# Another split of the C products between VectorE and GpSimd, stage by stage, in a Mamba, expert and recurrence block

## The reference

```python
def step(h, t):
    u_t, d_t, B_t, C_t = t
    dA = jnp.exp(d_t[:, :, None] * A)
    h = dA * h + (d_t * u_t)[:, :, None] * B_t[:, None, :]
    y_t = jnp.einsum('bdn,bn->bd', h, C_t)
    return (h, y_t)
```

## Time and profile before

| | |
|---|---|
| median of 3 runs | 1953.68 us (1950.45 to 1956.26) |
| profiled execution, its time | 1957.38 us |
| profiled execution, its span | 1955.6 us |
| VectorE busy | 1661.3 us (85% of the span) |
| TensorE busy | 1608.4 us (82%) |
| ScalarE busy | 1537.7 us (79%) |
| GpSimd busy | 1358.5 us (69%) |
| granted TensorE clock, mean | 0.938 of full |

### The profile page before, as it was taken

One profiled execution on the slowest core, in us unless ns is written; L12 is line 12 of the kernel. 1 busy time (PEld: TensorE's weight loads), 2 busy tenths in 40 slices (PEclk: granted clock), 3 DMA queues, 4 the chain that ended last, 5 costly groups with the idle time before them and its releaser, 6 DMA issues. The chain is left out here.

```text
span 1955.6 us, 24773 instructions
## 1 busy us (share of the span) xinstructions
PE 1608.4 (82%) x6097; PEld 887.0 (45%) x6186; DVE 1661.3 (85%) x4204; ACT 1537.7 (79%) x3276; POOL 1358.5 (69%) x1209
## 2 busy tenths in 40 slices
PE   5788788879898988898898989898989986766653
PEld 2333344445454545454454545454545443444332
DVE  3889989899998999999999999999999998844431
ACT  5666778789897979898898989898998975465543
POOL 0234647488877787787778788777778777776665
PEclk8899899999999999999999999999999997997776
DMA  2000212023323223232323232322323232233232
GB/s 60 11 11 27 71 29 70 27 79 86 88 83 93 81 79 96 76 98 81 93 84 90 84 99 79 92 87 67 103 81 95 83 85 83 76 102 98 87 95 83
DMA packets 79901, 151.06 MB, mean 77 GB/s; under 512 B 20584, under 2 KB 46592, under 8 KB 79680
## 3 DMA queue, kind: packets, MB, share of 16 engines
q0 software_dynamic: 49152, 134.28, 24.0%
q1 hardware_dynamic: 29344, 14.65, 2.7%
q10 hardware_dynamic: 1248, 0.34, 0.1%
HBM read 145.01 MB, written 4.19 MB: 76 GB/s over the span
## 5 line engine op out<-in xcount | busy, mean ns | idle before, releaser
L1468 POOL DMA_INDIRECT rows<-in_experts,index x1024 | 981.9, 959 | 357.2 <-issue 288.8
L1354 DVE TENSOR_TENSOR_SCAN hp<-dA,fed_ps 128x1024 f32<-128x1024 f32 x256 | 583.7, 2280 | 7.7 <-issue 2.9
L784 PE MATMUL ysum<-hp,ident 128*128 128x512 f32 x1024 | 487.6, 621 | 4.0 <-DVE hp L1364 3.4
L1483 POOL TENSOR_TENSOR hp<-hp,c_row 128x1024 f32<-128x1024 f32 x112 | 264.8, 2364 | 219.7 <-ACT c_row L1044 178.0
L1027 ACT ACTIVATE dA<-delta,decay 128x511 f32<-128x511 f32 x512 | 334.7, 711 | 17.2 <-issue 15.4
L1338 DVE TENSOR_TENSOR fed_ps<-du,b_ps 128x1024 f32<-128x1024 f32 x256 | 313.7, 1225 | 39.2 <-PE b_ps L759 23.5
L1006 ACT ACTIVATE rows<-rows,coef 128x128 f32<-128x128 f32 x1024 | 311.1, 390 | 13.1 <-DVE coef L1274 13.1
L784 PEld LDWEIGHTS ysum<-hp,ident 128*128 128x128 f32 x1024 | 206.7, 202 | 219.4 <-issue 201.7
L934 ACT ACT_TABLE_LOAD x218 | 279.7, 1283 | 8.8 <-PEq L544 5.0
L717 PE MATMUL bank<-rows,ident 128*128 128x256 f32 x1024 | 251.2, 402 | 32.5 <-ACT rows L1006 32.5
L1267 DVE CUSTOM_DVE_ANT_0 rows<-rows,xn 128x128 f32<-128x128 f32 x1024 | 240.9, 298 | 39.5 <-DMA rows<-in_experts,index 39.1
(11 more groups left out here) (182 smaller groups left out, 2195.4 us busy)
## 6 DMA issues: line engine op xcount, KB each, us to landing
rows<-in_experts,index POOLq DMA_INDIRECT x1024, 2.7
x_in<-in_x SPq DMA_DIRECT2D x16, 256.0 KB, 4.1
x_res<-in_x SPq DMA_DIRECT2D x16, 256.0 KB, 4.7
y<-x SPq DMA_DIRECT2D x16, 256.0 KB, 2.7
rows<-in_taps SPq DMA_DIRECT2D x1, 512.0 KB
rows<-in_wq_t SPq DMA_DIRECT2D x1, 512.0 KB, 5.2
rows<-in_in_proj_t ACTq DMA_DIRECT2D x1, 256.0 KB
rows<-in_key_t SPq DMA_DIRECT2D x1, 128.0 KB, 5.2
```

The costliest lines, as they stand in the source:

```text
L784: mm = nc.tensor.matmul(ysum[:, j, :], ident[:], hp[:, BUFFER[k], j, :], start=(k == SUM_ORDER[0]), stop=(k == SUM_ORDER[-1]))
L1354: nc.vector.tensor_tensor_scan(flat, dA[:, n % NDA, :, :].rearrange("p a b -> p (a b)"), fed_ps[:].rearrange("p a b -> p (a b)"), 0.0, ALU ...
L1468: pool.indirect_dma_start(e.rows[:, t, h, :], None, A["experts"], bass.IndirectOffsetOnAxis(ap=e.index[:, t, h:h + 1], axis=0)).then_inc(e ...
L1483: pool.tensor_tensor(state, state, c_row[:, k % NCR, :].unsqueeze(1).to_broadcast([P, NH, T]), ALU.mult).then_inc(pool_read, 1)
```

## The change

The set of states whose product GpSimd forms becomes a function of the stage, on_pool(c). In stage 0 it holds 1 to 14; in stage 1 it is 3, 4, 5, 7, 8, 9, 11; in stage 2 it is 1, 3, 5, 7, 8, 9, 11; in stage 3 it is 1, 3, 5, 6, 7, 8, 9, 11, 13; in stage 15 it is 1, 3, 5, 7, 9; in stages 4 to 14 it stays as it was. The order of the y sums follows the set of the stage, and the counts on which engines wait are added up over the stages. Slots, buffers and all other steps stay.

```diff
 POOL_STATES = (1, 3, 5, 7, 9, 11, 13)
-DVE_STATES = tuple(n for n in range(NS) if n not in POOL_STATES)
-
-SUM_AT = [min(n + 1 + (n in POOL_STATES), NS - 1) for n in range(NS)]
-SUM_ORDER = sorted(range(NS), key=lambda n: (SUM_AT[n], n))
...
+POOL_AT = {0: (1, 2, 3, 4, 5, 6, 7, 8, 9, 10, 11, 12, 13, 14), 1: (3, 4, 5, 7, 8, 9, 11), 2: (1, 3, 5, 7, 8, 9, 11), 3: (1, 3, 5, 6, 7, 8, 9, 11, 13), 15: (1, 3, 5, 7, 9)}
+
+def on_pool(c):
+
+    return POOL_AT.get(c, POOL_STATES) if isinstance(c, int) else POOL_STATES
+
+def pool_count(c, n):
+
+    if isinstance(c, int):
+        earlier = sum(len(on_pool(k)) for k in range(c))
+    else:
+        earlier = c * len(POOL_STATES) + sum(len(on_pool(k)) - len(POOL_STATES) for k in range(LOOP_FROM))
+    return earlier + sum(k <= n for k in on_pool(c))
...
+def sum_at(c, n):
+
+    return min(n + 1 + (n in on_pool(c)), NS - 1)
+
+def sum_order(c):
+
+    return sorted(range(NS), key=lambda n: (sum_at(c, n), n))
...
         def multiplied(c, n):
 
-            if n in POOL_STATES:
-                return pool_read, at(c, len(POOL_STATES), POOL_STATES.index(n))
-            return read_out, at(c, len(DVE_STATES), DVE_STATES.index(n))
+            if n in on_pool(c):
+                return pool_read, pool_count(c, n)
+            return read_out, dve_count(c, n)
...
-                        for k in [x for x in SUM_ORDER if SUM_AT[x] == n]:
+                        order = sum_order(c)
+                        for k in [x for x in order if sum_at(c, x) == n]:
                             pe.wait_ge(*multiplied(c, k))
...
-                        if n in POOL_STATES:
-                            c, k = b[CORE], POOL_STATES.index(n)
+                        if n in on_pool(b[CORE]):
+                            c = b[CORE]
                             act.wait_ge(c_spread, at(c, NS, n))
 
-                            if k >= NCR:
-                                act.wait_ge(pool_read, at(c, len(POOL_STATES), k - NCR))
-                            elif later(c):
-                                act.wait_ge(pool_read, at(c - 1, len(POOL_STATES), len(POOL_STATES) + k - NCR))
-                            nc.scalar.activation(c_row[:, k % NCR, :], c_ps[:, 0, :],
+                            if later(c) or n > on_pool(c)[0]:
+                                act.wait_ge(pool_read, pool_count(c, n) - NCR)
+                            nc.scalar.activation(c_row[:, 0, :], c_ps[:, 0, :],
                                                  ACT.Copy).then_inc(c_kept, 1)
...
-                    if CORE in has and part == 2 and n in DVE_STATES:
+                    if CORE in has and part == 2 and n not in on_pool(b[CORE]):
...
-                    if CORE in has and part == 0 and n in POOL_STATES:
-                        c, k = b[CORE], POOL_STATES.index(n)
+                    if CORE in has and part == 0 and n in on_pool(b[CORE]):
+                        c = b[CORE]
                         pool.wait_ge(scanned, at(c, NS, n))
-                        pool.wait_ge(c_kept, at(c, len(POOL_STATES), k))
+                        pool.wait_ge(c_kept, pool_count(c, n))
```

More of the change, by code:

```diff
@@ L223, with dve_count, summed @@
 POOL_STATES = (1, 3, 5, 7, 9, 11, 13)
-DVE_STATES = tuple(n for n in range(NS) if n not in POOL_STATES)
-SUM_AT = [min(n + 1 + (n in POOL_STATES), NS - 1) for n in range(NS)]
-SUM_ORDER = sorted(range(NS), key=lambda n: (SUM_AT[n], n))
-def summed(n):
-    return SUM_ORDER.index(n)
+POOL_AT = {0: (1, 2, 3, 4, 5, 6, 7, 8, 9, 10, 11, 12, 13, 14), 1: (3, 4, 5, 7, 8, 9, 11), 2: (1, 3, 5, 7, 8, 9, 11), 3: (1, 3, 5, 6, 7, 8, 9, 11, 13), 15: (1, 3, 5, 7, 9)}
[7 more added lines that the diff above has]
+    return earlier + sum(k <= n for k in on_pool(c))
+def dve_count(c, n):
+    if isinstance(c, int):
+        earlier = sum(NS - len(on_pool(k)) for k in range(c))
+    else:
+        earlier = c * (NS - len(POOL_STATES)) + sum(len(POOL_STATES) - len(on_pool(k)) for k in range(LOOP_FROM))
+    return earlier + sum(k not in on_pool(c) for k in range(n + 1))
+def sum_at(c, n):
+    return min(n + 1 + (n in on_pool(c)), NS - 1)
+def sum_order(c):
+    return sorted(range(NS), key=lambda n: (sum_at(c, n), n))
+def summed(c, n):
+    return sum_order(c).index(n)
 def offset(phase, slot):
@@ L604, in multiplied @@
         def multiplied(c, n):
-            if n in POOL_STATES:
-                return pool_read, at(c, len(POOL_STATES), POOL_STATES.index(n))
-            return read_out, at(c, len(DVE_STATES), DVE_STATES.index(n))
+            if n in on_pool(c):
+                return pool_read, pool_count(c, n)
+            return read_out, dve_count(c, n)
         def c_used(c, n):
-            if n in POOL_STATES:
-                return c_kept, at(c, len(POOL_STATES), POOL_STATES.index(n))
+            if n in on_pool(c):
+                return c_kept, pool_count(c, n)
             return multiplied(c, n)
@@ L784, in iteration @@
                                 mm = nc.tensor.matmul(ysum[:, j, :], ident[:], hp[:, BUFFER[k], j, :],
-                                                      start=(k == SUM_ORDER[0]), stop=(k == SUM_ORDER[-1]))
+                                                      start=(k == order[0]), stop=(k == order[-1]))
                             mm.then_inc(y_sum, 1)
@@ L1350, in iteration @@
                         if before:
-                            dve.wait_ge(y_sum, at(c, NS, summed(before[-1])))
+                            dve.wait_ge(y_sum, at(c, NS, summed(c, before[-1])))
                         elif later(c):
-                            dve.wait_ge(y_sum, at(c - 1, NS, summed(max(k for k in range(NS) if BUFFER[k] == BUFFER[n]))))
+                            last = max(k for k in range(NS) if BUFFER[k] == BUFFER[n])
+                            dve.wait_ge(y_sum, at(c - 1, NS, summed(c - 1, last)))
                         nc.vector.tensor_tensor_scan(flat, dA[:, n % NDA, :, :].rearrange("p a b -> p (a b)"),
@@ L1477, in iteration @@
                     n, part = divmod(slot, TURN // NS)
-                    if CORE in has and part == 0 and n in POOL_STATES:
-                        c, k = b[CORE], POOL_STATES.index(n)
+                    if CORE in has and part == 0 and n in on_pool(b[CORE]):
+                        c = b[CORE]
                         pool.wait_ge(scanned, at(c, NS, n))
-                        pool.wait_ge(c_kept, at(c, len(POOL_STATES), k))
+                        pool.wait_ge(c_kept, pool_count(c, n))
                         state = hp[:, BUFFER[n], :, :]
                         pool.tensor_tensor(state, state,
-                                           c_row[:, k % NCR, :].unsqueeze(1).to_broadcast([P, NH, T]),
+                                           c_row[:, 0, :].unsqueeze(1).to_broadcast([P, NH, T]),
                                            ALU.mult).then_inc(pool_read, 1)
```

## The result

The changed kernel takes 1991.75 us in the median of 6 runs (1986.43 to 1997.19); the kernel before beside it takes 1956.6 (6 runs, 1950.45 to 1963.17). The ratio is 1.0154, 95% interval 1.0114 to 1.0193: 1.5% slower, against a forecast of 1940 us.

The account below looks back on a forecast made before the run. VectorE was taken to bound stages 0 to 3, while GpSimd can hold up work in stage 15. Stage terms -4.7 - 5.0 - 1.7 + 0 - 2.4 sum to -13.8 us, giving 1940 us; range 1930 to 1952.

Parts of the forecast that it names:

- Stages 4 to 14: Stages whose product set is unedited: assumed to keep their time, so no term in the sum.
- Stage 0, -4.7: Stage 0: seven products move to GpSimd; five count at 0.95 us each, -4.7 us; bounds 0 and -8.5.
- the 6.6 of all seven products: Stage 0: saving if all seven moved products kept their 0.95 us each; the forecast said not all stays.
- not 5: Stage 0, sign of a right forecast: the scan of state 15 comes some 5 us earlier.
- the early wait for b_ps: Stage 0: the feed's 3.73 us wait for TensorE's b_ps would lengthen by what products 2 and 4 save.
- Stages 1 and 2, -5.0 and -1.7: Moving product 13 to VectorE ends GpSimd collisions; stage 1 also shortens its tail: -5.0 us, and -1.7 in stage 2.
- Stage 3, 0: Products 6 and 8 to GpSimd: saving swallowed by a later b_ps wait, 0 us; bounds -1.9 and +1.2.
- Stage 15, -2.4: Products 11 and 13 to VectorE: +1.1, collision gone -2.7, shorter y-sum wait -0.8, so -2.4 us; GpSimd's lead becomes idle.
- rival (a): GpSimd's stage 15 lead carries through the drain: -9.5 instead of -2.4, -20.9 in all, 1932.8 us; chance 0.18.
- -13.8: Sum over stages 0, 1, 2, 3 and 15: -4.7 - 5.0 - 1.7 + 0 - 2.4 us.
- Rival (b): TensorE and ScalarE swallow VectorE's savings; only three collisions go: -4.9 us, 1948.8 us; chance 0.20.
- Rival (c): Slower: ScalarE's copies wait on the one C row in stages 0 and 3: +10.2 us, 1964; chance 0.09.

Follow-up runs that it names:

- e5: Changed kernel plus four tiny ScalarE copies at the start, its loop at place 813 instead of 808: 1953.5 us, ratio 0.9925 to the kernel before.
- e7: Kernel before plus seventeen tiny ScalarE copies at the start, its loop at 808 instead of 790, no product moved: 1995.7 us, ratio 1.0196.
- e1: Changed kernel with the second expert layer's first weigh one slot earlier in stages up to 14: 1962.4 us, ratio 0.999 to the kernel before.
- e9: Kernel before (old sets) with the weigh one slot earlier and twenty-two ScalarE copies, loop at 813: 1956.3 us.
- e12: Changed kernel (all new sets) with the weigh one slot earlier and four ScalarE copies, loop at 813: 1940.3 us.
- e11: Changed kernel with stage 3's old set, the weigh one slot earlier and eight ScalarE copies, loop at 813: 1994.4 us.
- e3: Kernel before with only stage 15's new set: 1968.1 us, ratio 0.9996 to the kernel before.
- e10: Kernel before with stage 15's new set alone, the weigh one slot earlier and twenty-two ScalarE copies, loop at 813: 1958.0 us.
- e6: Changed kernel with four ScalarE copies at the start and the weigh one slot earlier: 1938.4 us, ratio 0.9878 to the kernel before.
- e13: e11 with four tiny VectorE memsets at the start, VectorE's loop at 1090 instead of 1086: 1940.8 us, ratio 0.9864 to the kernel before.
- e14: e12 with four tiny VectorE memsets at the start, VectorE's loop at 1086 instead of 1082: 1997.5 us, ratio 1.0149 to the kernel before.

## Why the prediction was wrong

**Stages 4 to 14.** The failed step is the sentence that they keep their set "and, I take it, their time". It was never worked out; no rival had it. They lost 59 us in all: 63.8 in stages 6 to 13, with 4.7 gained in the others. Two things did it, neither of them a wait on the change's data. Nine more c_row copies in stages 0 and 3 made ScalarE's code 18 instructions longer ahead of the loop, which put the place of a second fetch on the first dA behind each jump (e5, e7). And the weigh met GpSimd's product (e1), by what trigger stays open. The prediction counted the copies' 0.58 us and not their code.

**Stage 0, -4.7.** From first scan to first scan 78.2 became 71.3, -6.9 (-6.1 between e9 and e12): about the 6.6 of all seven products. Two lines of DVE of after carry it:

```profile
107.53 2.29 DVE L1384 TENSOR_TENSOR_SCAN hp<-dA,fed_ps 128x1024 f32<-128x1024 f32 x1
...
114.48 1.23 DVE L1367 TENSOR_TENSOR fed_ps<-du,b_ps 128x1024 f32<-128x1024 f32 x1 [3.34 <-POOL du L1534]
```

The scan of state 15 begins 7.7 us earlier than before (115.2), not 5. The forecast let the early wait for b_ps swallow products 2 and 4. Only 2 stands ahead of that wait; VectorE formed product 4 at 70.38, behind the feed at 69.24. Nor was 2 swallowed: the 3.73 us of the earlier trace rows became 1.68 and 1.98, no more in all, and the later waits for b_ps up to the scan of state 15 fell from 2.1 to 1.1 us. The last feed waits 3.34 us, now for GpSimd's du, as GpSimd's queue is fuller.

**Stages 1 and 2, -5.0 and -1.7.** -6.9 and -3.1 in the two profiled executions, -6.7 and -1.3 between e9 and e12. The collisions of the earlier trace rows went as told; the forecast was some 2 us short in stage 1.

**Stage 3, 0.** Right on its own edit: the two waits for b_ps behind the moved products grew to 2.75 and 3.44 us, and e11 has the same time with the old set. Wrong on the stage, which took 5.3 us more (3.9 between e9 and e12), because what stages 0 to 2 saved meets ScalarE's chain to rr there. (The profiled execution of e3, with the old sets in stages 0 to 3, took 105.0 too, so this is not the only way to a longer stage 3.)

**Stage 15, -2.4, and the drain.** -7.1 in the two profiled executions, but -2.8 between e9 and e12 and -2.0 between e9 and e10: the forecast was about right, and some 4 us of the old 125.9 were not the set's: e9, with the old set, takes 121.3. Two collisions of before with products that were not moved (an off step of 2.12 us at 1628.51, a dot of 2.46 at 1641.10) are not in it; one at the weigh (1.99) has come in. The drain took 238.2 us in before and 237.3 in after: rival (a) is out, the lead turns idle as told (in after GpSimd waits 7.95 us for TensorE ahead of its fetch at 1730.93, and 4.14 us for an index at 1797.41).

**The sum and the rivals.** -13.8 was forecast, and with the loop's two causes away the sets give -14.3 (e9 to e12, without the copies). That this comes so near is in part luck: between the profiled executions of e9 and e12 stages 0 and 1 give 3.1 us more than forecast, and stage 3 takes 3.9 that were put at nothing. Rival (b) is out by stage 0, where VectorE kept what it saved. Rival (c) had the sign, and the 1964 of its price lies 28 us short; its mechanism is not what happened: in stage 0 no scan waits for dA.

The lock of which the Trainium skill, page SBUF — State Buffer, section SBUF: two separate sides, tells was left out of the sum beside the moved products, with the reason that VectorE runs almost only operations with an input in PSUM there. For the edited stages the trace agrees: the one collision with a product in stages 0 to 3 of after (score, 1.97 us) stands in stage 3 of before too (1.95). It was the rule that mattered in the loop, where small VectorE steps start within 0.5 us of a product that was not moved.

## What to carry to other kernels

In a hardware loop the stages that an edit does not touch are not safe from it: code added ahead of the loop moves the loop against the blocks in which code is fetched, so count the instructions that each engine has ahead of its loop, and look in the trace for idle time marked "issue" behind the jump. Where small VectorE steps end within a few tenths of a microsecond of a GpSimd product, the schedule stands at an edge; moving the step one slot, or shifting code by a few instructions that do nothing, tells an edge from a real cost. Before a change is judged by its time, move the loop's place, and compare kernels with the place the same: here the move alone turned 1.5% slower into 0.75% faster (e5), with the weigh moved out of the product's way into 1.2% faster (e6), and at the same place, with the weigh moved in both, the new sets are 16 us or 0.8% faster than the old (e9, e12).

## What was not expected of the hardware

The queue of code fetches is on the page. DMA view of the whole execution of after (packets, MB, share):

```profile
q8 instruction: 61, 1.00, 0.2%
q14 instruction: 105, 0.85, 0.1%
```

1.00 MB / 61 is 16 KB a packet and 0.85 MB / 105 is 8 KB, so the second queue brings code in packets of 8 KB. The kernel before has 96 packets on it, the shifted e5 100.

A VectorE step can lose to a GpSimd product whose record starts later than it: 663.42 against 663.83 in after. In e13 an index step 0.01 us ahead of a product was spared, so the recorded starts alone do not tell who will lose. And a place in VectorE's code that moves with the instructions ahead of it, with no jump near, cost 0.28 to 0.29 us of idle time in the even stages of e11 and e14; that is nothing by itself, and some 55 us by where it fell.
